# Second layer of a four-layer graph network on one core: blocks written out, a ring of three pairs, z in the gated rows

## The reference

```python
def _L1_gnn_ref(x, adj_a, adj_b, W_sa, a_sa, W_gcnb, b_gcnb, Wa, ba, Wb, bb):
    type_sum_a = adj_a @ x
    type_sum_b = adj_b @ x
    attn_a = jax.nn.sigmoid(jnp.concatenate([type_sum_a, x], axis=1) @ Wa.T + ba)
    attn_b = jax.nn.sigmoid(jnp.concatenate([type_sum_b, x], axis=1) @ Wb.T + bb)
    h = x @ W_sa
    s_left = h @ a_sa[0, :Hd]
    s_right = h @ a_sa[0, Hd:]
    scores = s_left[:, None] + s_right[None, :]
    e = jnp.where(adj_a != 0, jnp.exp(-jax.nn.leaky_relu(scores, 0.01)), 0.0)
    attn = e / (jnp.sum(e, axis=1, keepdims=True) + 1e-05)
    x_a = attn @ h
    x_b = adj_b @ (x @ W_gcnb) + b_gcnb
    return jax.nn.sigmoid(attn_a * x_a + attn_b * x_b)
...
x = _layernorm(x + _L1_gnn_ref(x, adj, adj, ...), axis=-1)
```

## Time and profile before

| | us |
|---|---|
| median of 3 runs | 857.46 (856.97 to 860.05) |
| the profiled execution: time | 860.67 |
| its span | 858.9 |
| granted clock, mean | 0.977 |
| PE busy | 788.6 (92%) |
| DVE busy | 457.4 (53%) |
| ACT busy | 331.8 (39%) |
| POOL busy | 103.0 (12%) |

### The profile page before, as it was taken

The page is one execution under the profiler, slowest core; times in us unless marked ns, Lnnn a source line. Parts: engine busy times, 40 slices in busy tenths (PEclk is TensorE's granted clock), DMA queues, the critical chain, the costliest instruction groups (busy, mean ns, idle before and its releaser), DMA issues.

```text
span 858.9 us, 12185 instructions
## 1 busy us (share of the span) xinstructions
PE 788.6 (92%) x4264; PEld 518.4 (60%) x4264; DVE 457.4 (53%) x956; ACT 331.8 (39%) x531; POOL 103.0 (12%) x200
## 2 busy tenths in 40 slices
PE   6868999999768999898997999999998999998997
PEld 5755766666466787777773654556654455465343
DVE  4574776667768668787874347212226021111655
ACT  3664655554136345454652214313335121222200
POOL 0010111111271001010101122000001100000343
PEclk9988999999879999999999999999999999999999
DMA  5669999998600000000002000000000000000011
GB/s 177 148 135 215 236 233 227 221 220 181 135 7 13 1 1 2 1 0 0 0 0 81 1 0 0 1 1 0 0 0 25 0 1 1 0 0 0 19 37 43
DMA packets 114870, 50.71 MB, mean 59 GB/s; under 512 B 103568, under 2 KB 109840, under 8 KB 114832
## 3 DMA queue, kind: packets, MB, share of 16 engines
q1 hardware_dynamic: 114832, 50.22, 26.7%
HBM read 22.95 MB, written 2.10 MB: 29 GB/s over the span
## 4 chain that ended last, share of the span: by engine, by line
PE 46%; issue 23%; SPq 13%; DMA 6%; ACT 4%; DVE 4%; POOL 4%; POOLq 0%; ACTq 0%; DVEq 0%
PE ps L631 10%; PE ps L751 10%; PE ps L729 8%; PE ps L779 7%; SPq L348 6%; SPq L341 5%; DMA adjf<-in_adj 4%; PE ps L760 3%; PE ps L716 3%; PE ps L519 2%; ACT adjb L816 2%; POOL x L461 2%; PE ps L542 1%; SPq L333 1%; DMA turned<-pl 1%
## 5 line engine op out<-in xcount | busy, mean ns | idle before, releaser
L631 PE MATMUL ps<-adjT,x 128*128 (+1 forms) x768 | 173.5, 379 | 7.9 <-DVE x L1299 4.2
L631 PEld LDWEIGHTS ps<-adjT,x 128*128 128x128 f16 x768 | 71.7, 98 | 93.2 <-issue 5.8
L572 PE MATMUL ps<-sup,turned 128*128 128x512 f16 x256 | 89.2, 396 | 11.5 <-DMA turned<-pl 10.7
L656 PE MATMUL ps<-H_hi,es_hi 128*128 128x258 f32 x256 | 76.3, 298 | 9.5 <-DVE es_lo L1040 6.0
L1040 DVE TENSOR_TENSOR hh_lo<-hf,hh_hi 128x512 fp32r<-128x512 f32 x32 | 22.2, 692 | 116.6 <-ACT hf L986 116.6
L751 PE MATMUL ps<-adjT,G 128*128 x384 | 83.6, 379 | 0.4 <-ACT hf L986 0.4
L656 PE MATMUL ps<-H_hi,es_lo 128*128 128x258 f32 x256 | 72.4, 283 | 0.0
L656 PE MATMUL ps<-H_lo,es_hi 128*128 128x258 f32 x256 | 72.3, 282 | 0.0
L574 PE MATMUL ps<-sup,turned 128*128 128x256 f16 x256 | 72.1, 282 | 0.0
L751 PEld LDWEIGHTS ps<-adjT,G 128*128 128x128 f16 x384 | 37.2, 98 | 45.4 <-issue 0.9
L887 ACT ACTIVATE es_hi<-tm 128x1024 fp32r<-128x1024 f32 x32 | 33.9, 1059 | 76.5 <-DVE tm L1217 63.2
(11 more groups left out here) (201 smaller groups left out, 1453.3 us busy)
## 6 DMA issues: line engine op xcount, KB each, us to landing
adjf<-in_adj SPq DMA_DIRECT2D x32, 512.0 KB, 5.7
x<-in_x SPq DMA_DIRECT2D x4, 512.0 KB, 7.9
out<-adjf SPq DMA_DIRECT2D x16, 128.0 KB, 1.7
adjf<-in_L_gnn_W SPq DMA_DIRECT2D x1, 1024.0 KB, 5.3
W1f<-in_L_gnn_W SPq DMA_DIRECT2D x1, 512.0 KB, 3.7
adjf<-in_L_gnn_W SPq DMA_DIRECT2D x1, 512.0 KB, 3.9
we<-in_L_gnn_edge_w SPq DMA_DIRECT2D x1, 256.0 KB, 3.8
w0x<-in_L_gnn_weight SPq DMA_DIRECT2D x1, 256.0 KB, 6.9
```

The source lines that it names most:

```text
L572: ins = mm(bank(6 + u), PT(HI, u)[:, jt, :], sup[:, jt, :], start=(jt == 0), stop=False, skip_group_check=True)
L631: ins = mm(bank(4 + f), x16[:, part, jt, f * P:(f + 1) * P], adj(b, jt), start=(jt == 0 and part == HI), stop=(jt == T - 1 and part == LO))
L656: ins = mm(bank(k, D + 2), es[p][:, jt % RE, k * P:(k + 1) * P], H[q][:, jt, :], start=(jt == 0 and (p, q) == (HI, HI)), stop=(jt == T - 1 ...
```

## The change

The ring grows from two pairs to three (RE = 6, DEEP = 3). ef is gone: the second exp is written over tm, linked behind the first. z is g4 itself; the wait for the sigmoid before g4 is written again moves from joined to neighbours. attend waits for z bank by bank at the first source tile, instead of for all four. All blocks are straight code on PE, ACT and DVE. At the end of a block, DVE does edge_scores(b+1, 1), edge_low(b+1, 1) and edge_scores(b+1, 2) ahead of joined(b), and ACT does edge_exp(b+1, 2) as well behind edge_exp(b+1, 1). sigmoid and residual of the block before come at pairs 3 to 6 instead of 2 to 5.

```diff
--- before.py
+++ after.py
@@ -86,7 +86,8 @@
     SLOPE = 0.01
     XS = 2048.0
     TOP = 16384.0
-    RE = 4
+    RE = 6
+    DEEP = RE // 2
     AB = 4
     PAIRS = T // 2
     G_BANK = (6, 7, 4, 5)
@@ -214,12 +215,11 @@
         main1 = ExitStack()
         nb = sb(main1, "nb", [P, 2, CB], BF16)
         tm = sb(main1, "tm", [P, RE, CB])
-        ef = sb(main1, "ef", [P, RE, CB])
         es = pair(main1, "es", [P, RE, CB])
         g4 = sb(main1, "g4", [P, TB, D])
         gate = sb(main1, "gate", [P, TB, 2])
         rz = sb(main1, "rz", [P, TB])
-        z = sb(main1, "z", [P, TB, D])
+        z = g4
         main1.close()
         lay1.close()
 
@@ -648,12 +648,12 @@
             def attend(b, pair):
 
                 pe.wait_ge(es_lo, b * PAIRS + pair + 1)
-                if pair == 0:
-                    wait_from(pe, z_ready, b * TB)
                 for jt in (2 * pair, 2 * pair + 1):
                     for k in range(TB):
+                        if jt == 0 and b:
+                            pe.wait_ge(z_ready, (b - 1) * TB + k + 1)
                         for p, q in ((HI, HI), (HI, LO), (LO, HI)):
-                            ins = mm(bank(k, D + 2), es[p][:, jt % RE, k * P:(k + 1) * P], H[q][:, jt, :],
+                            ins = mm(bank(k, D + 2), es[p][:, (b * T + jt) % RE, k * P:(k + 1) * P], H[q][:, jt, :],
                                      start=(jt == 0 and (p, q) == (HI, HI)), stop=(jt == T - 1 and p == LO))
                 ins.then_inc(e_used, 1)
 
@@ -681,8 +681,7 @@
             pe.wait_ge(H_ready, 2)
             for k in range(AB):
                 pe.wait_ge(adjT_landed[k], 16 * (T // AB))
-            block1(0)
-            with pe.Fori(1, B) as b:
+            for b in range(B):
                 block1(b)
             pe.drain().then_inc(l1_done, 1)
 
@@ -881,12 +880,11 @@
 
             def edge_exp(b, pair):
 
-                n, s = b * PAIRS + pair, slice(2 * pair % RE, 2 * pair % RE + 2)
+                n, s = b * PAIRS + pair, slice(2 * (b * PAIRS + pair) % RE, 2 * (b * PAIRS + pair) % RE + 2)
                 act.wait_ge(tm_ready, 2 * (n + 1))
-                wait_from(act, e_used, n + 1 - RE // 2)
-                run(es[HI][:, s, :], tm[:, s, :], ACT.Exp, scale=SLOPE - 1.0)
-                wait_from(act, es_lo, n + 1 - RE // 2)
-                run(ef[:, s, :], tm[:, s, :], ACT.Exp, scale=SLOPE - 1.0).then_inc(ef_ready, 1)
+                wait_from(act, e_used, n + 1 - DEEP)
+                own.link(run(es[HI][:, s, :], tm[:, s, :], ACT.Exp, scale=SLOPE - 1.0))
+                run(tm[:, s, :], tm[:, s, :], ACT.Exp, scale=SLOPE - 1.0).then_inc(ef_ready, 1)
 
             def gates(b):
                 act.wait_ge(g_ev, (b + 1) * TB)
@@ -908,29 +906,26 @@
             def block1(b):
 
 
-                for pair in range(2, PAIRS):
-                    if not (isinstance(b, int) and b == 0) and pair - 2 < TB:
-                        sigmoid(b - 1, pair - 2)
+                for pair in range(DEEP, PAIRS):
+                    if b and pair - DEEP < TB:
+                        sigmoid(b - 1, pair - DEEP)
                     edge_exp(b, pair)
                     if pair == 6:
                         for f in range(KD):
                             agg_high(0, b, f)
                 gates(b)
-                if not (isinstance(b, int) and b == B - 1):
+                if b < B - 1:
                     edge_exp(b + 1, 0)
                 gated(b)
-                if not (isinstance(b, int) and b == B - 1):
+                if b < B - 1:
                     edge_exp(b + 1, 1)
+                    edge_exp(b + 1, 2)
 
             act.wait_ge(p1_lo, P1_SPLITS)
-            edge_exp(0, 0)
-            edge_exp(0, 1)
-            block1(0)
-            with act.Fori(1, B - 1) as b:
-                own.enter(b - 1, TB)
+            for pair in range(DEEP):
+                edge_exp(0, pair)
+            for b in range(B):
                 block1(b)
-            own.leave(B - 2)
-            block1(B - 1)
 
             def conv_high(layer, t, scale):
 
@@ -1212,24 +1207,25 @@
 
                 j0 = 2 * pair
                 own.link(ts(nb[:, :, :], adjT[:, bass.ds(b, 1), j0:j0 + 2, :].rearrange("p a j c -> p (a j) c"), -1.0, -FAR, ALU.add, ALU.mult))
-                wait_from(dve, ef_ready, b * PAIRS + pair + 1 - RE // 2)
+                wait_from(dve, es_lo, b * PAIRS + pair + 1 - DEEP)
                 for jt in (j0, j0 + 1):
-                    stt(tm[:, jt % RE, :], slrow[:, bass.ds(b * CB, CB)], ex[:, jt, 0:1], nb[:, jt % 2, :],
+                    stt(tm[:, (b * T + jt) % RE, :], slrow[:, b * CB:(b + 1) * CB], ex[:, jt, 0:1], nb[:, jt % 2, :],
                         ALU.add, ALU.max).then_inc(tm_ready, 1)
 
                 dve.wait_ge(tm_ready, 2 * (b * PAIRS + pair + 1))
 
             def edge_low(b, pair):
-                n, s = b * PAIRS + pair, slice(2 * pair % RE, 2 * pair % RE + 2)
+                n, s = b * PAIRS + pair, slice(2 * (b * PAIRS + pair) % RE, 2 * (b * PAIRS + pair) % RE + 2)
                 dve.wait_ge(ef_ready, n + 1)
-                wait_from(dve, e_used, n + 1 - RE // 2)
-                low(es[LO][:, s, :], ef[:, s, :], es[HI][:, s, :]).then_inc(es_lo, 1)
+                wait_from(dve, e_used, n + 1 - DEEP)
+                low(es[LO][:, s, :], tm[:, s, :], es[HI][:, s, :]).then_inc(es_lo, 1)
 
             def neighbours(b):
 
                 for k in range(TB):
                     n = b * TB + k
                     dve.wait_ge(g_mm, n + 1)
+                    wait_from(dve, sig_ready, n + 1 - TB)
                     own.link(tt(g4[:, k, :], bank(G_BANK[k], D), brow[:, :], ALU.add))
                     tt(gate[:, k, :], ps[:, G_BANK[k], D:D + 2], tile(ex, n)[:, 2:4], ALU.add).then_inc(g_ev, 1)
 
@@ -1248,7 +1244,6 @@
                 for k in range(TB):
                     n = b * TB + k
                     dve.wait_ge(gated_ready, n + 1)
-                    wait_from(dve, sig_ready, n + 1 - TB)
                     stt(z[:, k, :], bank(k, D), rz[:, k:k + 1], g4[:, k, :], ALU.mult, ALU.add) \
                         .then_inc(z_ready, 1)
                 dve.wait_ge(z_ready, (b + 1) * TB)
@@ -1263,18 +1258,15 @@
                 if k == TB - 1:
                     normed(T + n, k % 2, tile(x, n))
 
-            LINKS1 = PAIRS + TB + 3 + 2 * TB
-
             def block1(b):
 
 
-                last = isinstance(b, int) and b == B - 1
-                for pair in range(2, PAIRS):
+                last = b == B - 1
+                for pair in range(DEEP, PAIRS):
                     edge_scores(b, pair)
-                    if pair > 2:
-                        edge_low(b, pair - 1)
-                    if not (isinstance(b, int) and b == 0) and pair - 2 < TB:
-                        residual(b - 1, pair - 2)
+                    edge_low(b, pair - 1)
+                    if b and pair - DEEP < TB:
+                        residual(b - 1, pair - DEEP)
                     if pair == 6:
                         for f in range(KD):
                             agg_low(0, b, f)
@@ -1288,10 +1280,10 @@
                         conv_low(1, t, dsc[:, t:t + 1])
                 else:
                     edge_low(b + 1, 0)
-                joined(b)
-                if not last:
                     edge_scores(b + 1, 1)
                     edge_low(b + 1, 1)
+                    edge_scores(b + 1, 2)
+                joined(b)
 
             def conv_low(layer, t, scale):
 
@@ -1305,12 +1297,9 @@
             edge_scores(0, 1)
             edge_low(0, 0)
             edge_low(0, 1)
-            block1(0)
-            with dve.Fori(1, B - 1) as b:
-                own.enter(b - 1, LINKS1)
+            edge_scores(0, 2)
+            for b in range(B):
                 block1(b)
-            own.leave(B - 2)
-            block1(B - 1)
             for k in range(TB):
                 conv_low(1, 4 + 2 * k, dsc[:, 4 + 2 * k:5 + 2 * k])
                 conv_low(1, 5 + 2 * k, dsc[:, 5 + 2 * k:6 + 2 * k])
```

## The result

The changed kernel takes 871.56 us (median of 6 runs, 869.23 to 875.36), the kernel before 857.22 in the same measurement: a ratio of 1.0171, interval 1.0141 to 1.0200, so 14.7 us slower (12.1 to 17.1). Forecast was 872.7.

What follows compares the result with a forecast made beforehand. PE was taken to bound the kernel (busy 92% of the span), with DVE next. Boundaries +15.0, blocks -5.9, small parts -0.5 and clock +6.6 gave +15.2 us: 872.7 us against the median 857.46, range 866.0 to 879.0.

Steps and rivals of the forecast that it cites:

- joined behind three more steps: Block boundaries: attend(b+1, 0) starts 12.74 us after attend(b, 7), PE idles 6.3 us; +15.0 us over three boundaries.
- The lead of 0.6 us at agg_low: Block boundary: edge_scores(b+1, 0) starts 0.6 us earlier, since ACT gets to agg_hi sooner; counted within the 12.74 us.
- The ring: Blocks 1 to 3: with three pairs no es_lo wait, each block 33.6 us; -5.9 us, bounds 0 and -5.9.
- PE gains nothing: the boundary rows hold no loop gap: Loops written out: no gain on PE; the small waits DVE loses in looped blocks are in the -5.9 us.
- Bank by bank: attend(b+1, 0) at boundaries: without it PE would wait 1.2 us longer, for the fourth z; already in the sum.
- The end of the layer: Last block: agg_low comes 0.6 us earlier and moves the end of the layer, -0.6 us.
- The clock: After each boundary's idle PE's granted clock falls: 2.2 us each, +6.6 us in all, between 0 and 8.8.
- The sum: Whole kernel: 15.0 - 5.9 - 0.5 + 6.6 = +15.2 us; against the median 872.7 us, slower by 1.8%.
- (1): PE's clock stays up after the boundary idles: +8.6 us, 866.1 us; chance 0.06.
- (2): Deeper ring gives nothing in the blocks, DVE or residual(b-1, 3) staying the limit: 878.6 us; chance 0.06.
- (3): Boundaries: DVE leaves block b early enough to hide z within PE's own 6.4 us: 847.1 us; chance 0.07.
- the fourth: Boundaries: the 0.6 us lead is absent and bank waits or ACT's gated rows bite: up to 877.6 us; chance 0.1.

Runs made afterwards that it cites:

- PE at work: Changed kernel with 28 matmuls of 512 columns, into a bank nobody reads, on PE ahead of attend(b, 0) of blocks 1 to 3: 867.62 us, ratio 1.0101.
- second dose: Changed kernel with joined(b) behind edge_scores(b+1, 1), ahead of edge_low(b+1, 1) and edge_scores(b+1, 2): 851.42 us, ratio 0.9903 to the kernel before.
- first dose: Changed kernel with joined(b) one step earlier, behind edge_low(b+1, 1) and ahead of edge_scores(b+1, 2): 868.25 us, ratio 1.0103 to the kernel before.

## Why the prediction was right, step by step

- **joined behind three more steps: right, and shown.** Boundaries of 12.9 us where 12.74 were worked out, idle of 6.4 for 6.3, +15.5 us for +15.0. The two doses and the run with joined put back show it to be the cause. Some 0.1 of the missing 0.15 is the link: the exps start 1.10 us apart, not 0.97 as in the earlier trace rows, and the second lasts 1.06, so a pair takes 2.16 where I took 2.11, twice per boundary (2.16 and 2.14 in the first).

```profile
302.14 1.06 ACT L886 ACTIVATE es_hi<-tm 128x1024 fp32r<-128x1024 f32 x1 [2.65 <-DVE tm L1212]
303.24 1.06 ACT L887 ACTIVATE tm<-tm 128x1024 f32<-128x1024 f32 x1
```

- **The lead of 0.6 us at agg_low: right.** agg_low starts at 299.04, 25.3 us after attend(0, 0) at 273.72; before it was 303.67 - 277.71 = 26.0. The step of the residuals, ahead of it in blocks 1 to 3, costs nothing: those blocks have no gap.
- **The ring: right in the sum, too simple in the cause.** Blocks 1 to 3 would take 33.6 us but for the clock, as worked out (the runs with PE at work and with the second dose show 33.60). The 5.9 us stood under the ring, with the loop's small waits in them at no price of their own. The runs split them: straight code alone gives 2.7 of them, the deeper ring with the exps in place the rest, and only if es_lo of pair 1 doesn't stand behind joined. "PE gains nothing: the boundary rows hold no loop gap" was wrong for the old order, where straight code also took 1.1 us off the boundaries; in the changed kernel they are set by DVE's longer chain, so it didn't show.
- **Bank by bank: right.** 1.17 us a boundary for the 1.2 worked out.
- **The end of the layer: right in sign.** -1.1 us for -0.6. From the last attend to the wait for agg_lo in the third layer it is 22.7 to 22.9 us in the six runs whose blocks have no es_lo wait, and 23.3 to 23.6 in the four others. I did not test it apart, so its cause is not shown.
- **The clock: right mechanism, term too large.** Taken at 2.2 us a boundary from the mean of six rows; in the profiled execution it is 1.35 (34.95 less 33.60), 3.9 in all for 6.6. Its size isn't fixed: the three blocks of the first dose took 35.8, 36.25 and 34.95 us, that is 2.2, 2.65 and 1.35, after the same 4.5 us of idle. The Trainium skill's page "TensorE: Matmul & The Clock Gate", section "What's actually happening", says that the cold start varies between runs of one kernel. The trace of the first dose goes beyond that: its three numbers are from one execution. The section's ceiling of 1% of the span holds for what these restarts cost: 3.9 us are 0.5% in the changed kernel, and the first dose's 6.2 are 0.7%. Why the six rows gave more is open.
- **The sum.** The stage and its end came to +12.3 for +15.2 (the clock's 2.7 make most of the difference), the medians to +14.3. That 872.7 lies so near 871.56 owes something to luck: some 2 us of the medians' distance lie outside the stage, in no place that the two executions show, and make up for most of what the clock term had too much. The experiments say the same. Each of the six versions with a ring of three comes out better against the changed kernel by ratio than by stage and end, by 2.4 to 4.7 us, so its ratio of 1.0171 may be some 3 us high. That is an estimate from the traces; it was not measured again.
- **The rivals.** The clock fell (1), the blocks did not keep their length (2), z was not hidden (3). Of the fourth, the lead was there, ACT's gated rows (310.50 to 312.19) lay beside DVE's scores, and PE shows no gap between banks. The third one's sum, though not its mechanism, nearly came true where joined was put back, since z was hidden by taking the steps from before it: boundaries of 6.3 us instead of the 6.4 it named, a ratio of 0.9904 where its 847.1 against 857.46 is 0.9879, since the rival reckoned with no late es_lo of pair 1. With the scores moved as well it is 0.9866.

## What to carry to other kernels

What stands ahead of a step in an engine's queue is its price, and that includes each wait for another engine in those steps: three steps of 4.9 us of DVE work cost 7.2 us (from 311.77 to 318.95 in the changed kernel), because the low among them waits 2.3 us for ACT. Before a deeper ring is filled at a boundary, ask which of the engine's steps frees what the bottleneck needs next, put that first, and use only waits, not the path, for running ahead. Count PE's own work at the boundary (6.1 to 6.5 us here): steps that fit in it are free, and what sticks out is paid in full and can cost the clock on top. Here the clock stayed after 1.1 us of idle and fell after 4.5 and more.

## What the runs showed of the hardware

Three things that I had not expected. The loss from a fallen clock after one and the same idle of 4.5 us varied from 1.35 to 2.65 us a time, and after 7.6 us, with all z awaited at once, from 1.3 to 2.3. The clock can fall after a shorter idle than the 3.2 us I had seen: in two executions, that with PE kept at work and the second dose, the first block had a mean clock of 0.95 and took 35.1 us, after the 2.0 us of idle ahead of it, with 3.4 us of work between it and another idle of 1.3 us. The clock was still 1.00 in the first microsecond of the block and fell then (0.64 from 274.5 to 276.0, 0.50 from 276.0 to 278.0 with PE kept at work). Five other executions of the same code there stayed at 1.00 and took 33.6.

```profile
273.69:308.78 35.09, 34.90 (x237) 29.51 (x241) 23.01 (x37) 14.55 (x16) 0.00 (x0) 0.95 0.00 1
```

And a loop costs DVE something even where its instructions are the same: straight code made four of the six stretches behind the first block shorter by 0.5 to 1.5 us. In the kernel before, DVE's four bias steps at L1233 start 0.70 us apart in the loop (from 350.63 on) and 0.53 outside it (from 307.92 on). With straight code they start 0.53 apart in that block too (from 348.33 on). The loops of PE, ACT and DVE were taken out together; the last block, which only PE ran in its loop, gained no more than 0.1 us. How much of the 3.8 is ACT's is not shown.
